# Queries and keys projected transposed, rotated in place and stacked by DMA through DRAM

## What is computed

```python
xn = layernorm(x)
# layer 0: differential attention, 16 heads with two 16-wide query maps each (32 maps), 8 key maps
q1, q2, k1, k2 = rope(...)                     # x[..., ::2], x[..., 1::2] rotated pairwise by position
a1 = softmax(q1 @ k1.T * scale + causal); a2 = softmax(q2 @ k2.T * scale + causal)
out = (a1 - lam * a2) @ v                      # then group norm over time and head, and Wo
# layer 1: plain causal attention, 16 heads of 16, biases, rope by halves
att = softmax(rope(q) @ rope(k).T * scale + causal) @ v @ Wo + bo
# experts: layer 0 top 2 of 16 and 2 shared ones, layer 1 top 1 of 8 with a capacity
x = x + s * silu(ffn(xn))
```

## Time and profile before

| | us |
|---|---|
| median of 3 runs | 560.18 |
| lowest, highest | 558.44, 562.69 |
| the profiled execution | 561.81 |
| its span, first to last instruction | 560.0 |

### The profile page before, as it was taken

The page is one execution under the profiler, slowest core; times in us unless marked ns, Lnnn a source line. Parts: engine busy times, 40 slices in busy tenths (PEclk is TensorE's granted clock), DMA queues, the critical chain, the costliest instruction groups (busy, mean ns, idle before and its releaser), DMA issues.

```text
span 560.0 us, 11368 instructions
## 1 busy us (share of the span) xinstructions
PE 469.0 (84%) x4080; PEld 323.8 (58%) x4080; DVE 357.3 (64%) x887; ACT 244.0 (44%) x459; POOL 201.3 (36%) x276
## 2 busy tenths in 40 slices
PE   3377799889999997799999997877888888789961
PEld 1264576556566663477776775465665656567640
DVE  3878738998988774245422348878877777741435
ACT  1043545366386655633343322234153544654312
POOL 2441310353677424013000067227345574520324
PEclk9769979998999999999999999977679898999995
DMA  8850006404420100423332262007000013000204
GB/s 273 265 183 1 2 3 235 141 18 111 126 76 4 42 2 3 133 67 104 105 104 76 66 195 78 2 0 298 4 2 11 18 43 106 3 3 2 72 23 150
DMA packets 28831, 44.11 MB, mean 79 GB/s; under 512 B 5729, under 2 KB 25057, under 8 KB 27489
## 3 DMA queue, kind: packets, MB, share of 16 engines
q1 hardware_dynamic: 26473, 37.09, 20.7%
q0 software_dynamic: 2304, 6.29, 3.5%
HBM read 28.13 MB, written 14.94 MB: 77 GB/s over the span
## 4 chain that ended last, share of the span: by engine, by line
PE 60%; DVE 24%; issue 5%; POOL 4%; ACT 4%; DMA 2%; POOLq 0%; SPq 0%; DVEq 0%; ACTq 0%
PE bank L943 9%; PE bank L965 6%; PE bank L749 6%; PE bank L838 5%; PE bank L737 5%; DVE work L1441 5%; PE bank L845 4%; PE bank L773 4%; PE bank L866 3%; PE bank L769 3%; PE bank L888 3%; PE bank L797 2%; ACT work L1030 2%; PE bank L794 2%; PE bank L950 2%
## 5 line engine op out<-in xcount | busy, mean ns | idle before, releaser
L1030 ACT ACTIVATE work<-bank 96x1024 bf16<-96x1024 bf16 (+5 forms) x187 | 107.6, 587 | 114.7 <-PE bank L749 47.8
L1441 DVE TENSOR_REDUCE work<-bank 128x4 f32<-128x512 f32 (+1 forms) x144 | 96.7, 686 | 41.4 <-PE bank L773 39.1
L1072 ACT ACTIVATE work<-bank 128x512 f32<-128x512 f32 x144 | 83.8, 597 | 72.0 <-PE bank L797 41.4
L749 PE MATMUL bank<-identb,work 128*96 128x128 bf16 x576 | 51.5, 245 | 21.1 <-DVE work L1369 8.7
L1198 POOL COPY work<-work 128x1024 bf16<-128x1024 bf16 (+1 forms) x16 | 19.5, 1218 | 116.4 <-DVE work L1425 116.4
L749 PEld LDWEIGHTS bank<-identb,work 128*96 128x96 bf16 x576 | 45.8, 144 | 25.7 <-issue 18.2
L737 PE MATMUL bank<-wqkv,xnT 128*128 128x512 f32 (+1 forms) x128 | 53.3, 548 | 3.6 <-ACT xnT L1030 1.5
L769 PE MATMUL bank<-neg_ts,identb 128*128 128x512 bf16 (+1 forms) x144 | 47.1, 327 | 7.9 <-DVE work L1441 6.3
L1748 DVE TENSOR_TENSOR work<-work,bank 128x176 f32<-128x176 f32 x47 | 15.8, 336 | 59.4 <-ACT work L1125 59.1
L965 PE MATMUL bank<-moe,work 88*128 (+1 forms) x188 | 50.7, 395 | 0.0
L845 PE MATMUL bank<-work,cst 128*32 128x256 f32 (+1 forms) x768 | 50.0, 330 | 0.0
(11 more groups left out here) (204 smaller groups left out, 846.1 us busy)
## 6 DMA issues: line engine op xcount, KB each, us to landing
moe<-w_in SPq DMA_DIRECT2D x9, 1056.0 KB, 6.7
x_slots<-wo SPq DMA_DIRECT2D x41, 128.0 KB, 1.9
work<-x_slots SPq DMA_DIRECT2D x31, 128.0 KB, 2.2
y_slots<-work SPq DMA_DIRECT2D x31, 128.0 KB, 1.7
moe<-f1a_in SPq DMA_DIRECT2D x1, 2048.0 KB, 8.8
moe<-f1b_in SPq DMA_DIRECT2D x1, 2048.0 KB, 13.3
moe<-x_slots SPq DMA_DIRECT2D x1, 1280.0 KB, 6.0
work<-x_in SPq DMA_DIRECT2D x4, 256.0 KB, 5.8
```

Of the source, the lines that this page charges most:

```text
L749: mm = nc.tensor.transpose(bfv(a.pj.bank(key))[0:STACK, u, :], stack[:, 8 * g + u].rearrange("p s d -> p (s d)"), identb[:, :])
L1030: return nc.scalar.activation(dst, src, ACT.Copy)
L1072: nc.scalar.activation(pT[at % 6], a.st.bank(w)[:, :], ACT.Exp, scale=SCALE)\
L1441: nc.vector.tensor_reduce(here[:, first:first + len(ms), half], a.s.bank((b, q))[:, :].rearrange("p (m s) -> p m s", s=n), AX_X, ALU.max, ...
```

## The change

The query and key projections are computed with the weights stationary and the tokens moving, so that the features lie on the partitions. A step is now a "pair" (b, g): in layer 0 three to a batch (g = 0 the keys, g = 1 and 2 sixteen query maps each), in layer 1 two (keys, queries). A pair is 128 partitions by 512 (first and second components of 16 maps, by 256 tokens); layer 0's keys are 128 by 256, with the weights' columns a second time in swapped order. Each pair goes through eight steps:

```diff
+PAIR_STEPS = ("project", "turn", "high", "rest", "mid", "low", "stage", "load")
-         tiles=(dict(project=(2, 3), turn=(2, 2, 3), sum=3, high=4, mid=4, parts=(9, 11, 12, 13, 13)),
-                dict(project=(6, 8), turn=(7, 7, 8), sum=8, high=13, mid=14, parts=(18, 19, 20, 21, 24))),
+         pairs=((1, 2, 3, 4, 5, 6, 7, 11), (4, 5, 6, 7, 8, 9, 10, 12), (9, 10, 11, 12, 13, 14, 15, 17)), kept=(13, 14),
...
-         tiles=(dict(project=(0, 1), turn=(0, 1, 2), sum=2, high=2, mid=2, parts=(5, 6, 7, 8)),
-                dict(project=(3, 5), turn=(4, 4, 5), sum=5, high=7, mid=7, parts=(10, 10, 11, 11))),
+         pairs=((0, 0, 1, 1, 1, 2, 2, 3), (2, 2, 3, 3, 3, 4, 4, 5)), kept=(4, 4),
```

PE projects, DVE rotates, ACT copies to the high part, POOL subtracts it, ACT copies to the mid part, POOL subtracts again for the low part, SP writes the three parts to DRAM and, when they have landed, reads them back as the six 16-row blocks. The transposes, the stack and the 96x1024 copies are gone. On SP:

```diff
+            def stage(a, b, g):
+                n, home = pair_at(a, b, g), parts_home(a, b, g)
+                sp.wait_ge(a.parted, n + 1)
...
+                    sp.dma_start(home.rearrange("k (c d) (m t) -> (d m) k c t", c=2, t=SEQ),
+                                 split[n % 2].rearrange("p k (c t) -> p k c t", c=2)).then_inc(a.staged[n % 2], 16)
+            def load(a, b, g):
+                n, home = pair_at(a, b, g), parts_home(a, b, g)
+                m0, m1 = pair_maps(a, g)
+                sp.wait_ge(a.staged[n % 2], 16 * (n // 2 + 1))
...
+                rows = qkT[a.n][b % a.kept][0:STACK, m0:m1, :].rearrange("p m t -> p (m t)")
+                for k, (r0, times) in enumerate(((0, 3), (3, 2), (5, 1))):
+                    if g == 0:
+                        src = home[0:times].rearrange("k r x -> (k r) x")
+                    else:
+                        src = home[k:k + 1].to_broadcast([times, DH, 16 * SEQ])
+                    sp.dma_start(rows[r0 * DH:(r0 + times) * DH], src).then_inc(a.loaded[b % 2][g], 16)
```

and on DVE and PE:

```diff
+            def turned(a, b, g):
...
+                if n >= 2:
+                    dve.wait_ge(a.parted, n - 1)
+                    dve.wait_ge(a.staged[n % 2], 16 * (n // 2))
...
+                if a.n == 0:
+                    for dst, k in ((o, 0), (t, 1)):
+                        last = nc.vector.tensor_tensor(dst, bank, rope_q[:, k, :].unsqueeze(1).to_broadcast([P, 2, SEQ]), ALU.mult)
...
+                nc.vector.tensor_tensor(o[:, 0, :], o[:, 0, :], t[:, 1, :], ALU.subtract)
+                nc.vector.tensor_tensor(o[:, 1, :], o[:, 1, :], t[:, 0, :], ALU.add).then_inc(a.turned, 1)
...
             def scores(a, b, q):
-                transposed(a, 2 * b + half, ms[-1])
+                for g in (0, 1 + ms[-1] // 16):
+                    pe.wait_ge(a.loaded[b % 2][g], 16 * PARTS * (b // 2 + 1))
```

More of the change, by code:

```diff
@@ L339, in program @@
         ys1_stored = [sem(f"ys1_stored{k}") for k in range(2)]
-        back0, back1 = ([sem(f"back{n}_{i}") for i in range(TILES)] for n in range(2))
+        back = [sem(f"back_{i}") for i in range(TILES)]
         dve_c, act_c, pool_c = sem("dve_chain"), sem("act_chain"), sem("pool_chain")
         s_cast = sem("s_cast")
+        chain_c = [sem(k) for k in ("turned", "high", "rest", "mid", "parted")]
+        staged = [sem(f"staged{k}") for k in range(2)]
         s_ones = sem("s_ones")
@@ L426, in attention_state @@
                 here = b * beats
-                for half, t in enumerate(c["tiles"]):
-                    i = 2 * b + half
-                    for beat, use in zip(t["project"], ("q", "kv")):
-                        put(here + beat, "project", (i, use))
-                    for k, beat in enumerate(t["turn"]):
-                        put(here + beat, "turn", (i, k))
-                    put(here + t["sum"], "sum", i)
-                    put(here + t["high"], "high", i)
-                    put(here + t["mid"], "mid", i)
-                    for beat, g in zip(t["parts"], a.order):
-                        put(here + beat, "part", (i, g))
+                for g, at in enumerate(c["pairs"]):
+                    for kind, beat in zip(PAIR_STEPS, at):
+                        put(here + beat, kind, (b, g))
+                for kind, beat in zip(("values", "kept"), c["kept"]):
+                    put(here + beat, kind, b)
                 for g, beat in enumerate(c["rows"]):
@@ L658, in _ @@
+            attention(attns[0], attns[0].steps)
             a0 = attns[0]
@@ new lines, in kept, with by_parity @@
+            def kept(a, b):
+                key, n = ("v", b), a.vheads * a.vw
+                a.pj.wait_full(dve, key)
+                bank = a.pj.bank(key)[:, 0:HALVES * n].rearrange("p (h n) -> p h n", h=HALVES)
+                if a.n == 0:
+                    nc.vector.tensor_copy(vals0[:, b], bank).then_inc(a.pj.free["dve"], 1)
+                    return
+                if b < 2:
+                    dve.wait_ge(a.ones, a.ones_all if b else 1)
+                def by_parity(x, c, w0):
+                    return x.rearrange("p (g c q) w -> p g c q w", g=a.pairs, c=2)[:, :, c, :, w0:w0 + DH]
+                bias = bv.rearrange("p (v w) -> p v w", w=DH)
+                for half in range(HALVES):
+                    vals = bank[:, half, :].rearrange("p (v w) -> p v w", w=DH)
@@ L1420, in high @@
[L1420 to L1432 removed]
+                last.then_inc(a.pj.free["dve"], 1)
@@ L1659, in attention @@
                         turned(a, *w)
[L1660 to L1665 removed]
+                    elif kind == "kept":
+                        kept(a, w)
                     elif kind == "max":
```

391 lines of the change are left out of this document (186 added, 205 removed).

## The result

| | before | after |
|---|---|---|
| time, median of 4 runs each | 561.4 us (558.4 to 563.8) | 694.1 us (692.1 to 695.2) |
| ratio, 95% interval | | 1.236 (1.230 to 1.242) |
| profiled execution, span | 560.0 us | 693.4 us |
| granted clock, mean | 0.927 | 0.818 |
| DMA moved | 44.1 MB | 65.9 MB |

The kernel became 133 us slower. The forecast was 645 us, 84 more than before; the direction and the mechanism were those of the forecast, the size lay above its range.

The account below looks back on a forecast made before the run. PE was taken to bound layer 0's attention, PE and DVE alternating layer 1's. To 561.8 us came +20 (ramp), +50 and +3 (layer 0), +12 (layer 1): 647, given as 645; own range 610 to 672, with rivals 1, 3, 4 550 to 675.

Parts of the forecast that it names:

- Engines and duration of a query load: Query loads' copy-led transfers run on 3 and 2 DMA engines, one fast, one slow: 15 us, 17 from issue; chance 0.45.
- The reading of 0.68 as 11/16: L627's 88-partition transfer, share 0.68, uses 11 of 16 engines: transfers are dealt out by outermost count, here 13.4 GB/s each.
- The start: Ramp: first stage behind fills, table loads and expert weights; first scores at 57 us, first exponential's at 80, +20.
- load 2: Second query load of a layer 0 batch; in the ramp it lands at 75 us, asked for at 71.
- Layer 0: PE waits 9 us for load 1 and 11 for rows; period 58.7 us against 42, +50, plus +3 from expert weights.
- Layer 1: Walk through layer 1's batches: query load lands at 31.5 us against 22, period 36 against 32.6; stage ends +12.
- the -1 of the table: Forecast difference from layer 1's first scores to the last output projection's wait for POOL: -1 us.
- The relief: Busy time lower by about 35 us on DVE, 50 on ACT, 25 on PE; gains of 10 to 12 us layer 0, 22 layer 1.
- Rival 1: Narrow query loads with all their engines at 26.3 GB/s last 12 us; 584 us in all; chance 0.20.
- Rival 2: Loads spread over all engines last 4 us and are hidden, so reliefs count; 533 us; chance 0.24.
- Rival 3: Narrow loads last 12 us but other engines run ahead of PE and hide most; no change, 560; chance 0.06.
- Rival 4: Slow because the chain turn, high, rest, mid, low crosses engines at one beat each; 575 to 600; chance 0.05.

Follow-up runs that it names:

- the kernel of 607.6 us: Against the changed kernel with one wide 96-row load per query pair: 41 fills as two transfers and all expert weights behind a batch's third load; 607.6 us, ratio 1.081.

## Why the prediction was right or wrong

**Engines and duration of a query load: right.** Forecast 15 + 1.9 us, a share of 0.2 and under 100 GB/s; measured 16.0 and 16.5 us, 0.15 to 0.20, 52 to 61 GB/s. One slow and one fast transfer was the choice between the ends: the transfer of two copies moves 25 GB/s an engine, near the fast end of 26.3, that of three 18 to 19, between 26.3 and 13.4. But the total was hit better than its parts, and that is luck: one transfer of 10 and one of 5 us, end to end, would leave 12 us without the three copies and 12 without the two, and these loads took 14.4 and 13.1. The reading of 0.68 as 11/16 carried the whole forecast; that it holds for a broadcast was the author's estimate before the runs, and so were the two rates: no run shows three copies at 13.4 GB/s an engine, the windows show 18 to 19, and 25 for two.

**The start: nearly right.** First scores forecast at 57, measured 57.3; load 2's landing 75 and 74.8; the first exponential's 80 and 84.3. Of this the fills and weights ahead of the first stage are 10.5 us, by the run that moves them.

**Layer 0: right in kind, 12 us short.** Forecast waits of 9 and 11 us a batch. Measured before first scores 1.4, 12.4 (7.2 and 5.2) and 9.1, before the rows' scores 16.9, 16.3 and 11.8: 68 us in place of 60. The rows' wait was taken too short, since PE arrives there 5.4, 7.3 and 7.0 us after the load and not 8, and with weights behind them the rows land later. The +3 for the weights measured about 5. The rest is more exposed waiting, some of it at a lower clock (0.82 from 84 to 317 us, 0.97 before).

**Layer 1: the step that failed, 30 of the 49 us.** "In each later batch the query load, issued at beat 5 plus some 3 us for stage and an f1 piece, lands at 31.5 us against the 22 us of beat 10: period 36 against 32.6." The periods were 43.2, 44.4 and 43.2 us. Without the wait a period was right, twelve beats of 2.2 us: 26.4 us in the walk, measured 26.2, 26.4 and 28.0. The wait was wrong: 9.5 us in the walk, measured 17.0, 18.0 and 15.2. In the terms of that sentence, for batches 1 to 3:

| | forecast | measured |
|---|---|---|
| from PE reaching beat 5 to the load's issue | 3 | 6.5, 9.1, 7.1 |
| from the load's issue to the first scores | 17 | 15.8, 16.6, 17.1 |
| PE's five beats from 5 to 10 (the cover) | 11 | 5.3, 7.7, 9.0 |

The first row is the stage, taken at 3 us: it took 6.2, 7.7 and 5.6 (503.82 to 510.05 in the first). It runs beside the keys' load and, in the first two, the f1 pieces. Which of them costs how much is open: with the f1 pieces behind, in the kernel with sooner pairs and narrow loads, it still took 6.3, 5.3 and 2.7.

The last row is the cover, taken in steps of a fixed 2.2 us. The five beats ahead of batch 2's first scores on PE, before and then after:

```profile
432.63 0.39 PE L802 MATMUL bank<-moe 99*128 99x256 bf16 x2
...
434.21 1.95 PE L737 MATMUL bank<-wqkv,xnT 128*128 128x256 f32 x4
...
437.01 0.94 PE L749 MATMUL bank<-identb,work 128*96 128x128 bf16 x8
...
443.42 0.40 PE L802 MATMUL bank<-work 99*128 99x128 bf16 x4
```

```profile
544.55 0.63 PE L857 MATMUL bank<-moe 99*128 99x256 bf16 x2
...
551.87 0.40 PE L857 MATMUL bank<-work 99*128 99x128 bf16 x4
```

Before, these beats took 10.7, 11.2 and 12.9 us, the 11 of the forecast. But four banks of transposes (L749, some 2 us) and a projection (L737, 1.8 us) lay in them, and the change takes out the first and moves the second ahead of beat 5. So the walk booked the transposes as relief and still counted on the time that they had filled. PE passes what is left with hardly a pause and stands when the load has hardly been issued. This is read from the two traces; no run changes the cover by itself.

Three periods are 130.8 us in place of 108, 23 of the 30 us. The other 7 lie behind the last batch's first scores: 63.9 us against 66.4 before, where the -1 of the table needs some 57. The relief that the walk had credited there did not come, and even with wide loads the stage got only 3 us shorter.

**The relief.** Busy time fell by 37 us on DVE and 45 on ACT (35 and 50 forecast), but by 12.5 on PE in place of 25. The transposes' 51.5 us are gone; the projections take 61.0 in place of 53.8, and the same scores and values (L824, L828, L849, L852, L894, L901) 282.5 in place of 259.5, with a mean granted clock of 0.818 against 0.927. That the clock is the reason for the latter is argued, not shown.

**The rivals.** Rival 1 (12 us a load, 584) fell: 16 us. Rival 2 (spread over all engines, 533) fell twice: the loads are narrow, and made wide they give 586, and 571 with everything else moved, not 533. Its error, as far as the wide kernels show it, is the booking of 34 us of relief as time. Rival 3 (hidden) fell with the 166 us of waits. Rival 4 (the chain crossing the engines) names what may be left at 571 to 574.

## What to carry to other kernels

Before costing a DMA by its bytes, look at how many engines it can use: a load whose largest transfer is led by a broadcast of three copies ran on three of 16 (3.2 by the share of 0.20) and took 16 us for 0.79 MB, and what stood behind it on the queue, even 8 KB, waited as long (15.6 and 19.4 us). When a transfer becomes longer than its cover, don't count the cover in steps of the mean period: read from the trace what the engines do in just those steps, take off what the change removes from them, and start the transfer where its own source has landed. Here that left 5 to 9 us of the 11, less 6 to 9 until the issue, so that nearly the whole load was exposed in each batch. Moving the load or its consumer mostly changed at which line the wait was seen (50.2 us of waits for scores became 41.9 of waits for rows); making the load shorter (longest wait for rows 4.4 us with one wide load, 16.9 in after), or moving bulk transfers away from in front of urgent ones (25.6 and 4.5 us), took most of it away.

## What the runs showed that was not expected

Small transfers found no way past large ones on SP's queue: 8 KB landed 19.4 us after issue behind a narrow load (15.6 with no weights behind them), and PE stood 25.6 us for it where four transfers of expert weights lay ahead, three of them of L627's slow kind. Issuing is not always cheap either: in the kernel of 607.6 us the two transfers that fill 41 tiles, behind a query load, held SP's queue for

```profile
41.78 10.79 SPq L635 DMA_DIRECT2D x_slots<-wo  x2
52.61 3.58 SPq L640 DMA_DIRECT2D moe<-w_in  x1
```

10.8 us, and a single transfer of weights behind them 3.6, where two otherwise take 0.95. It is not the number of rows alone: in the kernel with the weights spread one transfer of 24 such tiles took 0.44 us to issue at the start, and two with the other 17 tiles took 1.0. What holds the queue is open. And splitting one broadcast into six plain transfers, three issues more on the queue, made the kernel 100 us faster.
